# Decoder layer on one core: feature tiles of the memory stage turned by VectorE blocks and DRAM instead of TensorE, and another order of tile 1's attention chain

## What is computed

```python
# memory attention, on _layernorm(x); G = 4, so 8 of 32 query heads are used
q = (hidden @ Wq.T + bq).reshape(b, s, 32, 128)
sig_q = jax.nn.elu(q) + 1.0
q_sel = sig_q[:, :, ::G, :]
num = jnp.einsum('bshd,hde->bshe', q_sel, M)
den = jnp.einsum('bshd,hd->bsh', q_sel, z)[..., None] + EPS
out_heads = jnp.repeat(num / den, G, axis=2)
x = x + out_heads.reshape(b, s, H * D) @ Wo.T
# cross attention, on _layernorm(x): keys and values of context and x, 8 query heads per key head
attn = jax.nn.softmax(jnp.einsum('bqhgd,bkhd->bhgqk', q, k) * scale)
x = x + jnp.einsum('bhgqk,bkhd->bqhgd', attn, v).reshape(b, q_len, 4096) @ Wo
```

## Time and profile before

| | |
|---|---|
| median of 3 runs | 683.93 us (682.43 to 684.12) |
| the profiled execution | 682.47 us, its span 680.7 us |
| PE busy | 669.3 us, 98% of the span |
| DVE busy | 512.1 us, 75% |
| ACT busy | 402.3 us, 59% |
| POOL busy | 120.2 us, 18% |
| context, keys, weights of the memory | 0 to 68 us |
| 16 queries of the memory stage | 65.5 to 149.1 us |
| its tail, six outputs | 149.1 to 168.3 us |
| values of the latents | 168.3 to 191 us |
| products for keys and queries | 191 to 248 us |
| attention and experts | 248 to 680.7 us |

### The profile page before, as it was taken

How to read it: one execution, slowest core, us unless ns; L and a number is a source line. 1 busy time by engine, 2 the same in 40 slices (tenths; PEclk the granted TensorE clock), 3 DMA queues, 4 the chain that set the end, 5 groups by cost and what they waited for, 6 DMA issues and landing times.

```text
span 680.7 us, 11137 instructions
## 1 busy us (share of the span) xinstructions
PE 669.3 (98%) x3394; PEld 563.1 (83%) x3394; DVE 512.1 (75%) x1101; ACT 402.3 (59%) x1224; POOL 120.2 (18%) x132
## 2 busy tenths in 40 slices
PE   8999999999999999899999999999999999999997
PEld 7888888888888888688888888888888888888885
DVE  3774876778887887767776967677887676778887
ACT  4454754455553445577567865775876575555553
POOL 0197000000332311111011010110110000032422
PEclk9999999999999999899999999999999999999999
DMA  8997150001243656687867568867667683221101
GB/s 327 370 365 265 38 180 1 1 0 32 92 156 125 199 159 208 185 238 252 234 185 229 170 187 247 250 208 201 191 201 238 185 259 106 82 83 63 63 17 62
DMA packets 100676, 113.26 MB, mean 166 GB/s; under 512 B 6096, under 2 KB 72912, under 8 KB 100624
## 3 DMA queue, kind: packets, MB, share of 16 engines
q1 hardware_dynamic: 95696, 104.78, 49.6%
q10 hardware_dynamic: 4928, 7.87, 3.2%
HBM read 73.83 MB, written 38.80 MB: 165 GB/s over the span
## 4 chain that ended last, share of the span: by engine, by line
PE 89%; DVE 5%; issue 2%; ACT 2%; DMA 1%; DVEq 0%; SPq 0%; ACTq 0%
PE bank L1055 23%; PE bank L1125 23%; PE bank L873 15%; PE bank L1248 7%; PE bank L1027 6%; PE bank L1265 6%; PE bank L864 2%; ACT probs L1690 1%; PE bank L1274 1%; DVE oT L1874 1%; PE bank L1194 1%; PE bank L992 1%; PE bank L914 1%; PE bank L958 1%; DMA raw<-in_ctx 1%
## 5 line engine op out<-in xcount | busy, mean ns | idle before, releaser
L1125 PE MATMUL bank<-regA,oT 128*128 128x512 f32 x576 | 135.7, 391 | 1.6 <-DVE oT L1874 1.5
L1125 PEld LDWEIGHTS bank<-regA,oT 128*128 128x128 f32 x576 | 107.4, 188 | 25.8 <-DVE oT L1874 3.6
L1690 ACT ACTIVATE probs<-bank,negmax 128x128 f32<-128x128 f32 x256 | 90.2, 379 | 63.6 <-DVE negmax L2332 58.0
L1055 PE MATMUL bank<-xnT,forms 128*128 128x512 f32 x432 | 107.1, 392 | 0.0
L1055 PEld LDWEIGHTS bank<-xnT,forms 128*128 128x128 f32 x432 | 80.2, 188 | 16.2 <-DVE qbuf L2090 0.2
L1055 PE MATMUL bank<-regC,forms 128*128 128x512 f32 x324 | 82.5, 393 | 0.0
L1055 PEld LDWEIGHTS bank<-regC,forms 128*128 128x128 f32 x324 | 59.9, 188 | 12.0 <-DVE regC L1874 0.2
L873 PE MATMUL bank<-regC,xnT 128*128 128x512 f32 x256 | 68.0, 396 | 0.0
L1376 ACT CAST oT<-bank 128x512 fp32r<-128x512 f32 (+1 forms) x66 | 37.8, 577 | 48.2 <-PE bank L1265 42.4
L1248 PEld LDWEIGHTS bank<-k_ring,qbuf 128*128 128x128 f32 x512 | 62.4, 192 | 2.6
L1248 PE MATMUL bank<-k_ring,qbuf 128*128 128x128 f32 x512 | 62.5, 275 | 0.0
(11 more groups left out here) (214 smaller groups left out, 1160.6 us busy)
## 6 DMA issues: line engine op xcount, KB each, us to landing
q_dram<-qbuf SPq DMA_DIRECT2D x32, 512.0 KB, 3.5
qbuf<-q_dram SPq DMA_DIRECT2D x31, 512.0 KB, 5.8
turns_dram<-probs SPq DMA_DIRECT2D x88, 128.0 KB, 2.5
pT_raw<-turns_dram SPq DMA_DIRECT2D x22, 512.0 KB, 5.2
wq_raw<-in_L_xattn_Wq SPq DMA_DIRECT2D x14, 512.0 KB, 4.4
raw<-in_L_attn_Wo SPq DMA_DIRECT2D x6, 1024.0 KB, 8.3
raw<-in_L_xattn_Wo SPq DMA_DIRECT2D x12, 512.0 KB, 6.2
k_ring<-keys_dram SPq DMA_DIRECT2D x32, 128.0 KB, 5.0
```

Source lines behind the costliest of these rows:

```text
L1055: last = nc.tensor.matmul(k_bank[:, :], forms[:, p[1], a, i, c, :], right(b)[:, c, :], start=j == 0, stop=j == 5)
L1125: last = nc.tensor.matmul(bank[7][:, :], oT[:, a, h, :], wo_of(g, b, h), start=h == 0 and i == 0, stop=h == GH - 1 and i == 2)
L1690: last = nc.scalar.activation(dst, keys, ACT.Exp, bias=negmax[:, bb, p:p + 1], accum_out=rowsum[:, bb, p:p + 1])
```

## The change

Two parts.

**Memory stage.** Half tiles 0 to 13 of 16 are no longer transposed by PE. The bias addition writes `qb` by blocks of 32 columns, so that a DVE transpose of 32x32 blocks (`nc.vector.transpose` at the end of step i, of half tile i-1), four stores to DRAM and one load (`turn_sig` on SP) give the transposed features in `sig_raw`, in SBUF. ACT's high and DVE's low half of half tile s then come three steps behind its query (`sig_due`), and PE's output five steps behind it instead of four; the loops get one step more. Half tiles 14 and 15 still go by PE. The latent work, which follows the outputs, is in even steps instead of odd ones. The SP queue: `turn_sig(0)` and `turn_sig(1)` come ahead of the value weights, which are now loaded into another place (`wv_again`), then the first key weights, `turn_sig(2)` to `turn_sig(13)`, and only then the 2 MB of `wo_raw` and `k_raw`.

**Tile 1's chain** in `first_steps`. DVE: `turn(1, 0)` and `turn(1, 1)` ahead of `sum_u3(p + 1)`; `turned_low(1, ...)` ahead of `sum_22(p + 1)` and `turn(2, ...)`. ACT: `turned_high(1, ...)` ahead of `normalise(2, ...)`.

The core of the diff (views and places of the same kind are left out):

```diff
+        SIG_TURNED = 2 * NT - 2
+        def by_head(i, rows):
+            if i < SIG_TURNED:
+                return rows.rearrange("q (c m j) -> q m c j", c=P // SUB, m=4)
+            return in_blocks(rows)
...
+        def sig_due(i):
+            return [s for s in range(2 * NT) if s + (3 if s < SIG_TURNED else 2) == i]
...
         def output_in(i):
-            return (i - 4) // 2 if i >= 4 and (i - 4) % 2 else None
+            return (i - 5) // 2 if i >= 5 and (i - 5) % 2 else None
...
# SP
+            def turn_sig(i):
+                sp.wait_ge(sig_turned, i + 1)
+                for a in range(P // SUB):
+                    sp.dma_start(sig_dram[i % 2, :, :, a, :].rearrange("c j n -> j c n"),
+                                 sig_turns(i)[a * SUB:(a + 1) * SUB, :].rearrange("j (c n) -> j c n", n=4 * SUB))\
+                      .then_inc(sig_stored, 16)
+                sp.wait_ge(sig_stored, 64 * i + 64)
+                if i >= 2:
+                    sp.wait_ge(sig_lo, i - 1)
+                sp.dma_start(sig_raw(i), sig_dram[i % 2, :, :, :, :].rearrange("c j a n -> (c j) (a n)"))\
+                  .then_inc(sig_loaded, 16)
+            turn_sig(0)
+            turn_sig(1)
             sp.wait_ge(tr_done, tr("wo", MH - 1) + 1)
-            load_wkv(0, 1)
-            sp.dma_start(wo_raw, wo_rows[:, 0:GH, :]).then_inc(wo_loaded, 16)
+            for i in range(2):
+                sp.dma_start(wv_again[:, 2 * i:2 * i + 2, :], wv_rows[:, 2 * i:2 * i + 2, :])\
+                  .then_inc(wkv_loaded[0][i], 16)
...
             sp.dma_start(wq_raw[:, :, :], wk_rows[:, :, 0:2 * P]).then_inc(wq_loaded, 16)
-            sp.wait_ge(sig_tr_done, 2 * NT)
+            for i in range(2, SIG_TURNED):
+                turn_sig(i)
+            sp.wait_ge(wkv_lo, 3 * KC)
+            sp.dma_start(wo_raw, wo_rows[:, 0:GH, :]).then_inc(wo_loaded, 16)
+            sp.wait_ge(sig_tr_done, 2 * NT - SIG_TURNED)
             sp.dma_start(k_raw, wk_rows[:, :, 2 * P:4 * P]).then_inc(k_raw_loaded, 16)
...
# PE
             def sig_transposes(i):
                 pe.wait_ge(sig_scaled, i + 1)
-                if i >= 2:
-                    pe.wait_ge(sig_lo, i - 1)
+                pe.wait_ge(sig_lo, i - 1)
...
-                if i >= 4:
-                    memory_output(i - 4)
-                if 2 <= i < 2 * NT + 2:
+                if i >= 5:
+                    memory_output(i - 5)
+                if SIG_TURNED <= i - 2 < 2 * NT:
                     sig_transposes(i - 2)
...
# ACT
-                if i >= 2:
-                    tile, quad = divmod(i - 2, 2)
-                    act.wait_ge(sig_tr_done, i - 1)
+                for s in sig_due(i):
+                    tile = s // 2
+                    if s < SIG_TURNED:
+                        act.wait_ge(sig_loaded, 16 * s + 16)
+                    else:
+                        act.wait_ge(sig_tr_done, s - SIG_TURNED + 1)
                     if tile >= 4:
                         act.wait_ge(y_done, tile - 3)
-                    high(sigT[:, 0, 4 * quad:4 * quad + 4, (tile % 4) * P:(tile % 4 + 1) * P],
-                         sig_bank(i - 2)[:, :].rearrange("p (m n) -> p m n", m=4)).then_inc(sig_hi, 1)
+                    high(sigT_place(0, s), sigT_source(s)).then_inc(sig_hi, 1)
...
# DVE
-                        dve.wait_ge(sig_tr_done, i - 2)
+                        dve.wait_ge(sig_turned, min(i - 2, SIG_TURNED))
...
+                for s in sig_due(i):
+                    dve.wait_ge(sig_hi, s + 1)
+                    low(sigT_place(1, s), sigT_source(s), sigT_place(0, s)).then_inc(sig_lo, 1)
+                if 1 <= i <= SIG_TURNED:
+                    s = i - 1
+                    dve.wait_ge(sig_scaled, s + 1)
+                    if s == 0:
+                        dve.wait_ge(tr_done, tr("wqa", MH - 1) + 1)
+                    if s >= 2:
+                        dve.wait_ge(sig_stored, 64 * s - 64)
+                    nc.vector.transpose(sig_turns(s), sig[:, s % 3, :]).then_inc(sig_turned, 1)
...
# first_steps, ACT
                 summed_high(pair + 2, 1 - slot)
+                for bb in range(2):
+                    turned_high(1, bb)
                 normalise(2, 0)
                 normalise(2, 1)
-                for bb in range(2):
-                    turned_high(1, bb)
...
# first_steps, DVE
                 sum_11(p + 1)
-                sum_u3(p + 1)
                 turn(1, 0)
                 turn(1, 1)
+                sum_u3(p + 1)
...
                 summed_low(p + 2, 1 - slot)
+                turned_low(1, 0)
+                turned_low(1, 1)
                 sum_22(p + 1)
                 turn(2, 0)
                 turn(2, 1)
-                turned_low(1, 0)
-                turned_low(1, 1)
```

More of the change, by code:

```diff
@@ L271, in decoder_layer @@
         sig_tr_done = sem("sig_tr_done")
+        sig_turned = sem("sig_turned")
+        sig_stored = sem("sig_stored")
+        sig_loaded = sem("sig_loaded")
         den_summed = sem("den_summed")
@@ L389, in mm_bank, with sig_by_head, in_blocks, sig_turns @@
             return bank[2 + i % 2]
+        SIG_TURNED = 2 * NT - 2
[3 more added lines that the diff above has]
+            return in_blocks(rows)
+        def sig_by_head(i):
+            return by_head(i, sig[:, i % 3, :])
+        def in_blocks(rows):
+            return rows.rearrange("q (m c j) -> q m c j", c=P // SUB, j=SUB)
+        def sig_turns(i):
+            return rawk[:, 2048 + 512 * (i % 2):2560 + 512 * (i % 2)]
+        def sig_raw(i):
+            return rawk[:, 3072 + 512 * (i % 2):3584 + 512 * (i % 2)]
+        def sigT_place(a, s):
+            tile, quad = divmod(s, 2)
+            return sigT[:, a, 4 * quad:4 * quad + 4, (tile % 4) * P:(tile % 4 + 1) * P]\
+                .rearrange("p m (a i) -> p m a i", i=SUB)
+        def sigT_source(s):
+            if s < SIG_TURNED:
+                return sig_raw(s).rearrange("p (a m i) -> p m a i", a=P // SUB, m=4)
+            return sig_bank(s)[:, :].rearrange("p (m a i) -> p m a i", m=4, i=SUB)
+        def sig_due(i):
+            return [s for s in range(2 * NT) if s + (3 if s < SIG_TURNED else 2) == i]
         def sig_bank(i):
@@ L1011, in memory_step @@
                     wo_transposes(i + EARLY)
-                if output_in(i) and i < 2 * NT:
+                if output_in(i) and i < 2 * NT + 4:
                     latent_transposes(output_in(i) - 1)
-                if i == 2 * NT + 2:
-                    latent_transposes(output_in(i - 1) - 1)
             def memory_output(s):
@@ L1036, in latent_transposes @@
                 transpose_rows(tr("latent", t), xn[:, t % 2, :])
-            for i in range(2 * NT + 4):
+            for i in range(2 * NT + 5):
                 memory_step(i)
@@ L1452, in wkv_high @@
                         act.wait_ge(wkv_loaded[w][c // 2], 16 * loads[c // 2])
-                    high(wkv(0, w)[:, c, :], wkv_raw[:, raw, c, :]).then_inc(wkv_hi, 1)
+                    high(wkv(0, w)[:, c, :], raw[:, c, :]).then_inc(wkv_hi, 1)
             def ctx_high(t):
@@ L1564, in memory_step @@
                     for j in range(4):
-                        last = nc.scalar.mul(sig[:, s % 3, j * P:(j + 1) * P], sig[:, s % 3, j * P:(j + 1) * P],
-                                             rden[:, s % 2, j:j + 1])
+                        head = sig_by_head(s)[:, j, :, :]
+                        last = nc.scalar.mul(head, head, rden[:, s % 2, j:j + 1])
                     last.then_inc(sig_scaled, 1)
-            for i in range(2 * NT + 4):
-                if i < 2 * NT + 2:
+            for i in range(2 * NT + 5):
+                if i < 2 * NT + 3:
                     memory_step(i)
                 if i in (2 * NT, 2 * NT + 1):
-                    wkv_high(0, wkv2, (1, 2), 1, (2 * (i % 2), 2 * (i % 2) + 1))
-                if output_in(i) and i < 2 * NT:
+                    wkv_high(0, wkv2, (1, 2), wv_again, (2 * (i % 2), 2 * (i % 2) + 1))
+                if output_in(i) and i < 2 * NT + 4:
                     latent_high(output_in(i) - 1)
-                if i == 2 * NT + 2:
-                    latent_high(output_in(i - 1) - 1)
             def save_latent_values(t):
@@ L1907, in wkv_low @@
                     dve.wait_ge(wkv_hi, n + c + 1)
-                    low(wkv(1, w)[:, c, :], wkv_raw[:, raw, c, :], wkv(0, w)[:, c, :]).then_inc(wkv_lo, 1)
+                    low(wkv(1, w)[:, c, :], raw[:, c, :], wkv(0, w)[:, c, :]).then_inc(wkv_lo, 1)
             for t in range(NT):
@@ L1938, in _ @@
             x_moments(0)
-            wkv_low(1, wkv1, KC, 1)
+            wkv_low(1, wkv1, KC, wkv_raw[:, 1, :, :])
             def x_low(k, t):
@@ L2037, in _ @@
             dve.wait_ge(kv_written[1], kv_count(1, 16))
-            for i in range(2 * NT + 4):
-                if i < 2 * NT + 2:
+            for i in range(2 * NT + 5):
+                if i < 2 * NT + 3:
                     memory_step(i)
-                if i == 2 * NT:
```

(13 more changed lines are left out.)

30 lines of the change are left out of this document (14 added, 16 removed).

## The result

The changed kernel takes 684.06 us (median of 22 runs, 682.24 to 685.94), the kernel before 682.46 (22 runs beside them, 680.11 to 685.05). The ratio is 1.0025, with a 95% interval of 1.0015 to 1.0035: **1.7 us slower**. The forecast was a gain of 0.2 with a range of 679 to 690. The time lies in the range and within the 0.3% called "within", but the loss is real: its interval of 1.0 to 2.4 us leaves out both zero and the forecast gain. The way there differs from the one that was worked out: the term for the memory stage, +3.7 us, measured +6.4.

What follows compares the result with a forecast made beforehand. PE bounds the memory stage before; with transposes added, DVE's line (12.33 us a pair) was to bound it. Memory stage +3.7 and tile 1's chain -3.9 sum to -0.2 us: 683.7 us, range 679 to 690.

Steps and rivals of the forecast that it cites:

- the term for the memory stage: Memory stage: its end comes at 172.0 instead of 168.3, +3.7 us (+1 to +7).
- DVE's line, not PE's, sets the steps: Memory-stage query steps: two steps take 12.33 us on DVE, against 11.4 on PE.
- The first rival: Memory stage: DVE and ACT keep up, PE stays the bound, -6.1 - 3.9, total 674; chance 0.08.
- The trip through DRAM is hidden: Steady memory steps: storing and loading a turned tile takes 7.3 us (6.2 to 9.3), within 9.7 available.
- The rival in which it binds every step: Memory steps: DRAM trip exceeds 9.7 us; at 10.5, 690; chance 0.20 together with the case where only the front pays.
- The stall at tile 2: Front of the memory stage: tile 2's load lands late behind weights, holding DVE's line once, 2.1 us (0.5 to 4).
- the weights are in near 91, tile 2's pieces near 92: SP queue in the front: 1.5 MB of weights delay tile 2's stores, putting its load near 95.2, wanted at 93.1.
- The tail: End of memory stage: addition 15 at 154.4, 4 us PE wait ahead of tile 14's transposes, stage end 172.0.
- the wait at 165.8 hides all but about 0.3: Memory tail: PE runs at half clock after idling, but a later wait for a residual tile leaves 0.3 us cost.
- The outputs are only moved, one step later: Memory stage on PE: delaying the outputs adds no PE work, while removed transposes save 6.1 us.
- Tile 1: Tile 1's chain: the 2.8 us PE gap and part of the half clock go, -3.9 us (-4.4 to -1.5).
- The rival that the gap only moves: Tile 1's chain: reordering moves the gap to tile 2, half of the 3.9 stays, 685.7 to 687; chance 0.12.

Runs made afterwards that it cites:

- the run with the early transpose: Changed kernel with DVE transposing half tile i-2 mid-step instead of i-1 at its end, halves four steps behind the query; 687.98 us, ratio 1.0076.
- the memory stage alone: Changed kernel with the old order in `first_steps`, so only the turned memory stage remains; 687.22 us, ratio 1.0067.
- The last run: Changed kernel, weights behind the sixth tile, output 9 ahead of query 15, DVE's tail reordered, PE's latent transposes 4 and 5 one output later; 676.59 us, ratio 0.9923.
- the kernel with the chain alone: Kernel before with only the new order of tile 1's chain in `first_steps`; 678.83 us, ratio 0.9947.
- the runs with the tail moved: Changed kernel with step 14's residual work behind step 15's addition, 683.46 us; later runs add late weights, 679.90, and output 9 ahead of query 15, 679.59.
- the run with the clock held up: Changed kernel with filler transposes of the identity on PE, 34 ahead of query 15 and 22 ahead of half tile 14's transposes; 682.42 us, ratio 1.0005.
- the one with output 9 moved: Changed kernel with step 14's residual work behind step 15's addition, weights behind the sixth tile, PE's output 9 ahead of query 15; 679.59 us, ratio 0.9959.
- residual work behind step 15, weights late: Changed kernel with step 14's residual work behind step 15's addition and features, 1.5 MB of weights issued behind the sixth tile; 679.90 us, ratio 0.9969.
- the weights late alone: Changed kernel with the 1.5 MB of weights issued behind tile 5 instead of ahead of tile 2; 680.07 us, ratio 0.9965.
- the run with only the key weights late: Changed kernel with only the 0.5 MB of key weights issued behind the sixth tile, value weights left in place; 681.61 us, ratio 0.9995.

## Why the prediction was right or wrong

- **DVE's line, not PE's, sets the steps: right.** 12.33 us a pair predicted, 12.23 measured, PE's work 11.4. Its step with the transpose (4.39) measured 4.37. The first rival, with DVE and ACT keeping up, is out, and the run with the early transpose shows why busy time misleads here: 0.62 us of work cost 1.04 in that place and 0.32 in another. The Trainium skill (VectorE: DVE Perf Modes, Rules for kernel authors) would have such a transpose on TensorE; the memory stage alone at +4.6 us agrees with it. The last run, with the same fourteen transposes on DVE, is no slower than the kernel with the chain alone, so most of those 4.6 us came from what lay beside the transposes, not from the transposes.
- **The trip through DRAM is hidden: right in this kernel, and its price was set too high.** 7.3 us predicted; in the front, for the second tile, SP issued the stores at 81.47 and the load at 84.56, and the load takes 2.6 to land (median of 14), so about 6. The rival in which it binds every step has no row: only one high cast waited for it. In the runs with the tail moved it does come out, for the last turned tiles (0.93 to 2.2 us on ACT).
- **The stall at tile 2: right in place and cause, half its size.** 2.1 predicted, 4.6 measured on DVE, 4.1 in time. The step that failed is the term "the weights are in near 91, tile 2's pieces near 92". By the DMA issues the last weights, issued at 85.93, took 6.8 and were in near 92.7, and the four pieces took another 2.0 instead of 1: they were in DRAM at 94.72, 8.2 us after SP began to issue them. The load behind them took 2.8, against 3.4 predicted. From addition 5 (90.81, predicted 91.2) to addition 15 (156.44) it took 65.6, predicted 63.2: of the 2.7 us by which the stage was short, this is 2.4.
- **The tail: its end nearly right, its inside not.** From addition 15 to the first latent product it took 174.74 - 156.44 = 18.3, predicted 172.0 - 154.4 = 17.6. The wait ahead of tile 14's transposes was 2.46 and not 4, since PE came there only at 157.7 instead of 154.1: addition 13, which lets query 15 in, stood at 143.95 and not at 142.0, and behind PE's wait of 3.74 for it, which the prediction has only as a start time, query 15 took 4.29 instead of 2.77. And the term "the wait at 165.8 hides all but about 0.3" of the clock failed: the clock fell twice, and the run with the clock held up won 1.4.
- **"The outputs are only moved, one step later": the step with a price that wasn't looked for.** It puts the residual work into even steps, among them the seam between queries 14 and 15. The prediction counted it in the pair and didn't ask whom it stands ahead of. The order of the tail, in the main DVE's, is worth 2.5 to 3 us (the last run against the one with output 9 moved).
- **Tile 1: right.** -3.9 predicted, -3.6 measured alone, -3.7 by PE's landmarks on both sides of it in that trace, -4.1 in the changed kernel's, of which 0.5 is the memory stage's lead; by the way described: the gap gone, the clock 1.00 behind it, a new wait of 0.6 for low halves of the output. The rival that the gap only moves is out.
- **The second key weights:** no wait for them shows, as forecast.
- **The sum.** Stage +6.4 instead of +3.7, to the scores another +0.1, around tile 1 -4.1 instead of -3.9 (the reordering 3.6, the lead 0.5), last stores -1.0 instead of nothing: +1.4 instead of -0.2. That it missed by no more was luck: no term of the prediction has the lead or the stores, and without them the kernel would have been slower by another 1.5 us.

## What to carry to other kernels

Work moved off the bounding engine is paid for where it lands: read how long the receiving engine's line is with its waits for others, and where in that line the new instruction stands (0.62 us of work cost 1.04 behind a round trip and 0.32 ahead of it). Put no bulk load ahead of the first small transfers of a chain in the same queue. Where a loop's order is shifted by a step, go through its last iterations by hand: an engine in order can finish there what nobody wants yet, and one with slack in the middle has none at the end.

## What the hardware showed unexpectedly

**Small stores behind a bulk load.** Four stores of 64 KB were in DRAM 8.2 us after the first issue with 1.5 MB ahead of them, 6.2 (86.61 to 92.80) with 1 MB. For the tile before, with nothing ahead, it was 3.1 from their issue to the load's. But with all the weights moved away, the same tile's four still took 4.8 (86.31 to 91.13), so not all of the 8.2 is the weights; why isn't known.

**Idle time and the clock.** By the timelines output 12 took 3.0 us at full speed. Behind PE's wait of 2.46 us in the changed kernel it took 4.58, and 4.57 behind one of 2.58 (residual work behind step 15, weights late). Behind 2.48 with the weights late alone it took 3.00, and 3.01 behind 2.02. In the last run, after waits of 1.57 and 0.34, it took 4.58 again. Ahead of query 15 a wait of 3.75 us was followed by a granted clock of 1.00 and a product at full speed in the run with only the key weights late, where one of 3.74 cost 1.5 in the changed kernel. So the length of the wait alone doesn't tell whether the clock falls. Nor is the price fixed: 1.6 in these falls, but behind a wait of 5.24 in the run with the early transpose the granted clock was 0.50 all through output 11, and it took 5.49, some 2.5 more.

**The last stores.** The two last stores of the output, of 128 KB each, are the same in all these kernels. By the DMA issues (columns as in the earlier trace rows) they landed in 2.4 us in the kernel before:

```profile
out_x<-qbuf SPq DMA_DIRECT2D x2, 128.0 KB, 2.4
```

and in the changed kernel:

```profile
out_x<-qbuf SPq DMA_DIRECT2D x2, 128.0 KB, 1.9
```

The end of the span follows their issue by 3.8 us there (676.94 to 680.7) and 2.8 here (679.34 to 682.1). The kernel with the chain alone has 2.5; the memory stage alone, late weights and the last run have 1.9, so it seems to come with the new memory stage and not with the time. It gave back 1.0 of what that stage cost. Why isn't known; the changed kernel has one more buffer in DRAM, but no run took that alone.
